# Layer 1's edge loop: the shrink of the running totals moved from VectorE to ScalarE, with reordered queues

## Chip, cores and metric

One core of a Trainium2 chip runs the whole kernel in one launch. The metric is the device time of one execution in microseconds (us); shorter is better. The kernel before takes 6182.91 us (median of 3 runs, 6182.76 to 6188.17).

## What is computed

The network has four layers, each a graph step and a feed-forward step, over 3125 nodes of width 256 and 50,000 edges sorted by destination. The change is in the edge part of layer 1's graph step, an attention over each node's incoming edges with 4 heads of 64 columns:

```python
e = x_l[src] + x_r[dst] + (ea @ W_e).reshape(-1, H, C)
e = jnp.where(e > 0, e, NEG_SLOPE * e)
logits = jnp.einsum('ehc,hc->eh', e, att)
m = jax.ops.segment_max(logits, dst, num_segments=N)
a = jnp.exp(logits - m[dst])
denom = jax.ops.segment_sum(a, dst, num_segments=N)
alpha = a / denom[dst]
out = jax.ops.segment_sum(x_l[src] * alpha[..., None], dst, num_segments=N)
```

The kernel does the maximum and the sums in one pass. It keeps a running maximum (a "top") and running totals per block of 128 destination nodes; when the top rises, the old total is multiplied by exp(old top - new top), its "shrink", before the new sum is added.

## The kernel before, in words

Edges come in 110 batches of 4 tiles of 128; a batch has two pairs of tiles, k = 0 and k = 1. `gat_edges` (L3294) writes one queue per engine with `skewed` (L1173): each engine goes through its list of steps once per iteration, and a step with lag n works on the batch of n iterations ago. An engine executes its list in the order in which it is written; semaphores tie the engines together. Layer 3 uses the same function with one head (`UNITS` is 1 there, 2 in layer 1).

The steps of one iteration before the change, by engine, with the batch that each works on where Q is the batch whose second top is raised:

- VectorE: `hot` (one-hot rows of two tiles, L1164, batch Q+3); tops of pair 0 (two reductions L3388, Q); `raise_first` (L3396, Q); join of pair 0 (L3637, Q+1); tops of pair 1 (L3388, Q); `raise_second` (L3403, L3405, L3408, Q), which writes the shrink exponents; join of pair 1 and both bends (L3637, L3642, Q+1); `add(0)` and `add(1)` (L3422, batch Q-1): four fused multiply-adds each, one per head, total[k] = total[1-k] * shrink + new sum; `late` (L3664, Q+1): the reductions that give the logits.
- TensorE: `turn_logits(1)` (L3464, L3467, Q), `add` (L3478, Q-1: the new sums), `spread` (L3484, L3486, Q: tops and logits spread over the edges), the edge products (L3627, L3628, Q+2), `turn_logits(0)` (Q+1), `turn` (L3449, Q+3).
- ScalarE: `shrinks` (L3513, Q), `weigh` (L3517, L3519, then sixteen multiplications L3528 with two copies L3531, Q), `turn` (L3508, L3509, Q+3), `flush` (L3544, L3545, Q-1).
- GpSimd: index cast and two one-hot tiles (L1154, L1156), four gathers (L1122), and the multiplication by `att` (L3659).

`spread` waits for `shrink_ready`, which `raise_second` raises; `weigh` waits for `spread_top`; `turn_logits(1)` waits for `topped`, since the tops of pair 0 must have read the two PSUM banks before they are filled again.

Of the kernel before, what the change touches and what calls it, by code (L numbers as in the profile page):

```python
# [12 lines left out]
ALU = mybir.AluOpType  # L13
ACT = mybir.ActivationFunctionType
AX = mybir.AxisListType

P = 128
# [11 lines left out]
BATCH = 4  # L29
# [157 lines left out]
def tiled(ap, width):  # L187
    return ap.rearrange("p (t d) -> p t d", d=width)
# [892 lines left out]
class Gather:  # L1081

    def __init__(self, s, net, placed, table, width, lo):
        self.net, self.placed, self.table, self.width, self.lo, self.n = net, placed, table, width, lo, placed.width - lo
# [61 lines left out]
    def hot_tiles(self, eng, q, i, b, tick):  # L1150
        eng.wait_ge(self.rec_loaded[b], i * 16 + 16)
        eng.wait_ge(self.hot_free, q + 1)
        eng.sem_inc(tick, 1)
        eng.tensor_copy(self.idx[b][:, :], self.column(b, self.placed.far)).then_inc(self.idx_ready, 1)  # L1154
        for k in range(BATCH // 2):
            ins = eng.tensor_scalar(at(self.onehot[b], k, P), self.net.columns[:, :], self.column(b, self.placed.near, k),  # L1156
                                    None, ALU.is_equal)
        ins.then_inc(self.hot_ready, 1)

    def hot_half(self, eng, q, i, b):  # L1160
        wide = [P, BATCH // 2, P]
        eng.wait_ge(self.rec_loaded[b], i * 16 + 16)
        eng.wait_ge(self.hot_free, q + 1)
        eng.tensor_tensor(tiled(self.onehot[b][:, :], P)[:, BATCH // 2:BATCH, :],  # L1164
                          self.net.columns[:, :].unsqueeze(1).to_broadcast(wide),
                          self.column(b, self.placed.near)[:, BATCH // 2:BATCH].unsqueeze(2).to_broadcast(wide), ALU.is_equal)\
            .then_inc(self.half_ready, 1)

    def wait_rows(self, eng, i, b):
# [2124 lines left out]
def gat_edges(net, name, heads, each, table, lo, logits_of, tops=None):  # L3294
# [11 lines left out]
    with ExitStack() as ctx:  # L3306
# [11 lines left out]
        power = [s.sb(f"power{b}", [P, KH]) for b in range(RING)]  # L3318
        weighted = s.sb("weighted", [P, BATCH * W])
        total = [s.sb(f"total{k}", [P, W]) for k in range(TWO)]  # L3320
        ps_hot = s.ps("ps_hot", [P, BATCH * P])
        ps_x = s.ps("ps_x", [P, TWO, 512])
        ps_row = s.ps("ps_row", [P, 2, 512])
# [11 lines left out]
        shrink_ready = s.sem("shrink_ready")  # L3335
        spread_top = s.sem("spread_top")
        eased = s.sem("eased")
        shrunk = s.sem("shrunk")
        powered = s.sem("powered")
        weighted_ready = s.sem("weighted_ready")  # L3340
# [21 lines left out]
        @block.vector  # L3362
        def _(dve):
            dve.memset(net.work[:, 0:NT * W], 0.0).then_inc(cleared, 1)
            dve.memset(top[:, :], -HUGE).then_inc(cleared, 1)
            dve.memset(total[TWO - 1][:, :], 0.0).then_inc(cleared, 1)
            if tops is not None:
                dve.memset(tops[:, :], -HUGE).then_inc(cleared, 1)
            dve.tensor_copy(ident[:, :], net.ident[:, :]).then_inc(ident_ready, 1)
            dve.tensor_scalar(minus[:, :], net.ident[:, :], -1.0, None, ALU.mult).then_inc(ident_ready, 1)  # L3370
            dve.tensor_scalar(fresh[:, :], placed.keep[:, :], -1.0, HUGE, ALU.add, ALU.mult).then_inc(fresh_step, 1)
            dve.sem_inc(topped, 2)
            dve.sem_inc(total_ready, TWO)
            dve.sem_inc(top_step, 1)
            logits.start_vector(dve)
            dve.wait_ge(cleared, 3 if tops is None else 4)
            dve.wait_ge(fresh_step, 1)

            def tops_of(k, h0):

                def step(q, i, b):
                    n = (q * TWO + k) * UNITS + h0 // 2
                    side = (k * UNITS + h0 // 2) % 2
                    dve.wait_ge(rows_turned, n + 1)
                    dve.wait_ge(topped, n + 1)
                    dve.sem_inc(dve_tick, 1)
                    w, c = min(2, heads - h0), k * heads + h0
                    dve.tensor_reduce(tile_top[:, c:c + w], tiled(ps_row[:, side, 0:w * PAIR], PAIR), AX.X, ALU.max)\  # L3388
                        .then_inc(topped, 1)
                return 4, step  # L3390

            def raise_first(q, i, b):
                n = q * TWO
                dve.wait_ge(topped, (n + 1) * UNITS + 2)
                dve.wait_ge(top_step, n + 1)
                dve.scalar_tensor_tensor(top_at(b, 0), top_at((b - 1) % RING, TWO - 1), fresh[:, bass.ds(n, 1)],  # L3396
                                         at(tile_top, 0, heads), ALU.add, ALU.max).then_inc(top_step, 1)

            def raise_second(q, i, b):
                n = q * TWO  # L3400
                dve.wait_ge(topped, (n + TWO) * UNITS + 2)
                dve.wait_ge(top_step, n + 2)
                dve.scalar_tensor_tensor(top_at(b, 1), top_at(b, 0), fresh[:, bass.ds(n + 1, 1)], at(tile_top, 1, heads),  # L3403
                                         ALU.add, ALU.max).then_inc(top_step, 1)
                dve.scalar_tensor_tensor(at(shrink[b], 0, heads), top_at((b - 1) % RING, TWO - 1), fresh[:, bass.ds(n, 1)],  # L3405
                                         top_at(b, 0), ALU.add, ALU.subtract).then_inc(shrink_ready, 1)
                dve.wait_ge(top_step, n + 3)
                dve.scalar_tensor_tensor(at(shrink[b], 1, heads), top_at(b, 0), fresh[:, bass.ds(n + 1, 1)], top_at(b, 1),  # L3408
                                         ALU.add, ALU.subtract).then_inc(shrink_ready, 1)

            def add(k):

                def step(q, i, b):
                    n = q * TWO + k
                    if k == 0:
                        dve.wait_ge(shrunk, q + 1)
                    dve.wait_ge(summed, n + TWO + 1)
                    dve.wait_ge(flushed, (n + 1) * FLUSH)
                    dve.wait_ge(total_ready, n + TWO)
                    for h in range(heads):  # L3420
                        own = slice(h * (each + 1), (h + 1) * (each + 1))
                        ins = dve.scalar_tensor_tensor(total[k][:, own], total[1 - k][:, own], shrink[b][:, k * heads + h:k * heads + h + 1],  # L3422
                                                       ps_s[:, k, own], ALU.mult, ALU.add)
                    ins.then_inc(total_ready, 1)
                return 5, step

            units = [tops_of(k, h0) for k in range(TWO) for h0 in range(0, heads, 2)]
            early, middle, late, find, hot = ((lag, lambda q, i, b, part=part: part(dve, q, i, b)) for lag, part in
                                              zip((3, 3, 3, 0, 1), logits.vector_steps()))
            ends = (add(0), add(1), late) if UNITS > 1 else (late, hot, add(0), add(1))  # L3430
            if UNITS > 1:
                skewed(dve, hot, *units[:UNITS], (4, raise_first), early, *units[UNITS:], (4, raise_second), middle, *ends)
            else:
                skewed(dve, find, *units, (4, raise_first), early, (4, raise_second), middle, *ends)

        @block.tensor
        def _(pe):
# [43 lines left out]
            def spread(q, i, b):  # L3481
# [3 lines left out]
                for m in range(BATCH):  # L3485
# [3 lines left out]
                ins.then_inc(spread_top, 1)  # L3489


            skewed(pe, *([(3, turn_logits(1))] if UNITS > 1 else []), (4, add), (1, lambda q, i, b: logits.blocks(pe, q)), (3, spread),
                   (1, lambda q, i, b: logits.tensor(pe, q, i, b)), (2, turn_logits(0)),
                   *([(2, turn_logits(1))] if UNITS == 1 else []), (0, turn))

        @block.scalar
        def _(act):
# [14 lines left out]
                act.wait_ge(shrink_ready, q * TWO + TWO)  # L3512
                act.activation(shrink[b][:, :], shrink[b][:, :], ACT.Exp).then_inc(shrunk, 1)  # L3513

            def weigh(q, i, b):
                act.wait_ge(spread_top, q + 1)
                act.activation(power[b][:, :], ps_fall[:, :], ACT.Relu).then_inc(eased, 1)  # L3517
                act.wait_ge(eased, q + 2)
                act.activation(power[b][:, :], power[b][:, :], ACT.Exp, scale=-1.0).then_inc(powered, 1)  # L3519
                g.wait_rows(act, i, b)  # L3520
                act.wait_ge(powered, q + 1)
                for k in range(TWO):
                    act.wait_ge(summed, q * TWO + k + 1)
                    for m in (2 * k, 2 * k + 1):
                        out = by_head(at(weighted, m, W), each + 1)
                        for h in range(heads):
                            lo = m * g.width + h * each
                            act.activation(out[:, h, 0:each], g.rows[b][:, lo:lo + each], ACT.Copy,  # L3528
                                           scale=power[b][:, m * heads + h:m * heads + h + 1])
                    ones = by_head(at(weighted, k, 2 * W), each + 1)[:, :, each]  # L3530
                    act.activation(ones, at(power[b], k, 2 * heads), ACT.Copy).then_inc(weighted_ready, 1)  # L3531
                act.wait_ge(weighted_ready, q * TWO + TWO)
                act.sem_inc(g.rows_free, 1)

# [9 lines left out]
                        act.activation(at(tops, blk, heads), top_at(b, k), ACT.Copy).then_inc(flushed, 1)  # L3544
                    act.activation(at(net.work, blk, W), total[k][:, :], ACT.Copy).then_inc(flushed, 1)  # L3545

            skewed(act, (3, shrinks), (3, weigh), (0, turn), (4, flush))


class L1Logits:  # L3550
# [943 lines left out]
```

## Time and profile before

| | us |
|---|---|
| median of 3 runs | 6182.91 |
| profiled execution | 6176.19 |
| its span, first to last instruction | 6174.6 |
| first to last shrink of layer 1 (109 steps) | 2226.7 to 3264.0 |

Busy share over the span: TensorE 81%, VectorE 66%, ScalarE 45%, GpSimd 50%. These are averages over stages with different limits; for this change only the stretch from 2227 to 3264 us counts. A timeline row gives the start, the time from the first to the end of the last of a run of equal instructions, the engine, the line, and in brackets how long the engine had been idle and what released it. Instructions of one engine overlap a little at their ends, so what one costs its engine is read from the distance between starts.

### The profile page before, as it was taken

The page shows a single profiled execution, that of the slowest core. Times are in us where ns is not written, and L with a number is a line of the kernel's source. Part 1 is how long each engine was busy: PE and PEld are TensorE (multiplying, and loading weights), DVE is VectorE, ACT ScalarE, POOL GpSimd, SP SyncE. Part 2 cuts the span into 40 slices and gives each one's busy share as a digit, 9 for nine tenths or more (in the row PEclk, how much of TensorE's full clock was granted, in tenths as well). Part 3 has the DMA queues.
Part 4 walks back from the last instruction along what each step waited for, and adds up shares of the span by engine and source line. Part 5 has one row for each costly group of instructions (what it writes and reads, how often), then busy time and mean ns, then how long its engine had stood idle before and what let it go on. Part 6 is the DMA issues. An engine that isn't in the chain of part 4 may idle for free. (4 is left out here: it accounts for less than half of the span.)

```text
span 6174.6 us, 119601 instructions
## 1 busy us (share of the span) xinstructions
PE 4978.6 (81%) x26396; PEld 3786.4 (61%) x26475; DVE 4081.7 (66%) x12578; ACT 2801.1 (45%) x8000; POOL 3087.3 (50%) x3487
## 2 busy tenths in 40 slices
PE   5720999998477779999993899969999997888695
PEld 4610677776354557777773677745657775777585
DVE  7771566665587779999996888754333336777612
ACT  0010777775115347777773111124533333787423
POOL 4787777775674068888880222213210002777221
PEclk9975999998696789999995999989989998999797
DMA  7521444445487222222231566544320002666453
GB/s 246 182 67 45 122 125 126 125 125 110 135 257 193 66 66 69 69 71 70 70 66 51 191 202 213 177 140 133 118 64 10 12 9 80 161 161 161 88 172 118
DMA packets 787155, 719.97 MB, mean 117 GB/s; under 512 B 349416, under 2 KB 693005, under 8 KB 786414
## 3 DMA queue, kind: packets, MB, share of 16 engines
q1 hardware_dynamic: 596376, 372.06, 21.2%
q0 software_dynamic: 120064, 280.26, 17.2%
q10 hardware_dynamic: 70486, 65.22, 3.0%
q8 instruction: 67, 1.10, 0.1%
q14 instruction: 162, 1.33, 0.1%
HBM read 520.74 MB, written 201.60 MB: 117 GB/s over the span
## 5 line engine op out<-in xcount | busy, mean ns | idle before, releaser
L1122 POOL DMA_INDIRECT l3e_rows<-table,l3e_idx x440 | 432.6, 983 | 733.8 <-DVE l3e_idx L1144 615.3
L1122 POOL DMA_INDIRECT l0e_rows<-table,l0e_idx x440 | 426.7, 970 | 154.3 <-issue 128.9
L1122 POOL DMA_INDIRECT l1e_rows<-table,l1e_idx x440 | 427.7, 972 | 121.4 <-issue 121.4
L890 POOL DMA_INDIRECT records_by_src<-l0n_rec_src,l0n_pos_at_src x390 | 398.0, 1020 | 115.4 <-issue 108.8
L3528 ACT ACTIVATE l1e_weighted<-l1e_rows,l1e_power 128x64 f32<-128x64 f32 x1760 | 442.6, 334 | 18.5 <-ACT l1e_power L3519 18.1
L1433 PE MATMUL l0e_ps_w<-l0e_wf,l0e_hidT 128*128 128x256 f32 x1760 | 435.3, 380 | 0.0
L3464 PE MATMUL l1e_ps_row<-net_ident,l1e_logit 128*128 128x128 f32 x1760 | 276.7, 280 | 82.4 <-DVE l1e_logit L3664 81.5
L1433 PEld LDWEIGHTS l0e_ps_w<-l0e_wf,l0e_hidT 128*128 128x128 f32 x1760 | 300.4, 191 | 63.0
L2168 ACT ACTIVATE l2fe_hT<-l2fe_ps_h,l2fe_own,l2fe_own 128x320 f32<-128x320 f32 x320 | 197.7, 618 | 310.7 <-PE l2fe_ps_h L2118 310.5
L3659 POOL TENSOR_TENSOR l1e_e<-l1e_e,l1x_att 128x512 f32<-128x512 f32 x220 | 313.8, 1446 | 29.2 <-DVE l1e_e L3642 21.5
L2827 ACT ACTIVATE l1fg_hT<-l1fg_ps_h,l1fg_b_cols 128x256 f32<-128x256 f32 x256 | 107.5, 471 | 458.0 <-PE l1fg_ps_h L2770 457.9
L1367 DVE SCALAR_TENSOR_TENSOR l0e_hidT<-l0e_ps_h,l0e_bf_low,l0e_raised 128x512 f32<-128x512 f32 x220 | 155.1, 746 | 227.6 <-ACT l0e_raised L1479 226.8
L2221 DVE SCALAR_TENSOR_TENSOR net_x<-l2fe_ps_y,l2fe_mix,net_x 128x256 f32 x200 | 96.7, 483 | 309.5 <-PE l2fe_ps_y L2130 309.5
L3388 DVE TENSOR_REDUCE l1e_tile_top<-l1e_ps_row 128x2 f32<-128x512 f32 x440 | 288.3, 685 | 16.1 <-PE l1e_ps_row L3467 3.5
L4057 PE MATMUL l2d_ps<-l2d_wide,net_work 128*128 128x512 f32 (+2 forms) x800 | 290.0, 518 | 8.6 <-DVE l2d_wide L4108 5.9
L3464 PEld LDWEIGHTS l1e_ps_row<-net_ident,l1e_logit 128*128 128x128 f32 x1760 | 191.6, 137 | 163.2 <-issue 110.7
L3478 PE MATMUL l3e_ps_s<-l3e_weighted,l3e_onehot 128*128 128x257 f32 x880 | 236.5, 414 | 53.1 <-ACT l3e_weighted L3531 52.6
L2951 POOL DMA_INDIRECT outputs<-l1fg_y,l1fg_target x64 | 66.3, 1035 | 404.0 <-DVE l1fg_y L2879 388.3
L3627 PE MATMUL l1e_ps_x<-l1x_xr,l1e_nodehot 128*128 x880 | 255.4, 392 | 2.8 <-ACT l1e_nodehot L3509 2.8
L2770 PE MATMUL l1fg_ps_h<-l1fg_xT,l1fg_w_in 128*128 128x256 f32 x1024 | 254.0, 381 | 0.8 <-issue 0.8
L3975 POOL DMA_DIRECT2D l2d_counts<-counts x192 | 107.1, 558 | 280.0 <-ACT l2d_wide L4167 139.9
L2784 PE MATMUL l1fg_ps_y<-l1fg_w_out,l1fg_hT 128*128 128x256 f32 x1024 | 241.5, 379 | 0.0
(857 smaller groups left out, 14927.0 us busy)
## 6 DMA issues: line engine op xcount, KB each, us to landing
counts<-l1f_total ACTq DMA_DIRECT2D x272, 128.0 KB, 4.4
l1fg_w_in<-in_L_ffn_W SPq DMA_DIRECT2D x32, 1024.0 KB
l1fg_w_out<-in_L_ffn_W SPq DMA_DIRECT2D x32, 1024.0 KB
records_by_dst<-l0n_blank_dst SPq DMA_DIRECT2D x5, 6512.0 KB
l3e_rec<-records_by_dst SPq DMA_DIRECT2D x110, 296.0 KB, 3.6
l2d_counts<-counts SPq DMA_DIRECT2D x208, 128.0 KB, 2.4
l2d_counts<-counts POOLq DMA_DIRECT2D x192, 128.0 KB
l3fg_w_in<-in_L_ffn_w SPq DMA_DIRECT2D x16, 1024.0 KB
```

Source lines behind the costliest of these rows:

```text
L890: pool.indirect_dma_start(self.to.records, bass.IndirectOffsetOnAxis(self.pos_at[b][:, j:j + 1], 0), at(self.rec[b], j, self.to.width), No ...
L1122: pool.indirect_dma_start(at(self.rows[b], k, self.width), None, self.table, bass.IndirectOffsetOnAxis(self.idx[b][:, k:k + 1], 0)).then_i ...
L1433: ins = pe.matmul(ps_w[:, k, m * D:(m + 1) * D], hidT[b][:, c * WIDE + (2 * k + m) * P:c * WIDE + (2 * k + m + 1) * P], at(wf2, c, D), sta ...
L2770: ins = pe.matmul(ps_h[:, n % HALVES, (m % 2) * SLICE:(m % 2 + 1) * SLICE], w_in[b][:, c * F + m * P:c * F + (m + 1) * P], at(xT[b], c, SL ...
L2784: ins = pe.matmul(ps_y[:, t, 0:D], hT[b][:, c * SLICE + t * P:c * SLICE + (t + 1) * P], at(w_out[b], c, D), start=c == 0, stop=c == FC - 1)
L3388: dve.tensor_reduce(tile_top[:, c:c + w], tiled(ps_row[:, side, 0:w * PAIR], PAIR), AX.X, ALU.max)\
L3464: pe.matmul(ps_row[:, side, lo:lo + P], logit[b][:, c:c + 1].to_broadcast([P, P]), net.ident[:, :], is_transpose=True, start=h == h0 and m ...
L3478: ins = pe.matmul(ps_s[:, k, 0:W], at(g.onehot[b], m, P), at(weighted, m, W), start=m == 2 * k, stop=m > 2 * k)
L3528: act.activation(out[:, h, 0:each], g.rows[b][:, lo:lo + each], ACT.Copy, scale=power[b][:, m * heads + h:m * heads + h + 1])
L3627: pe.matmul(out, at(self.nodehot[b], 2 * k + m, P), at(self.xr, self.block[k], D), start=True, stop=False)
L3659: pool.tensor_tensor(e, e, self.att[:, :].unsqueeze(1).to_broadcast([P, 2, D]), ALU.mult).then_inc(self.times_att, 1)
L4057: ins = pe.matmul(ps[0:k_in, n % 2, 0:width(g)], lhsT, wide[k % WIDE][:, 0:width(g)], start=t == 0, stop=False)
```

## The change

In layer 1 (`heads > 1`) the multiplication of a total by its shrink becomes a step of ScalarE, `fade(k)`: four activations, one per head, write total[1-k] * shrink into a new tile faded[k]. VectorE's `add(k)` is then one tensor_tensor over 260 columns, faded[k] + new sum. `fade(1)` stands at lag 4 between the two halves of the weighing of the next batch; `fade(0)` stands at lag 3 at the end of ScalarE's list. On VectorE the second join and both bends go directly behind the first join, ahead of the tops of pair 1; `add(0)`, `late`, `hot` and `add(1)` follow `raise_second` in this order. On TensorE the edge products go ahead of `spread`. GpSimd makes one one-hot tile instead of two and VectorE three instead of two. For one head (layer 3) the lists are the same as before.

```diff
-        for k in range(BATCH // 2):
+        for k in range(self.BY_POOL):            # BY_POOL = 1
...
-        eng.tensor_tensor(tiled(self.onehot[b][:, :], P)[:, BATCH // 2:BATCH, :],
+        eng.tensor_tensor(tiled(self.onehot[b][:, :], P)[:, self.BY_POOL:BATCH, :],
...
                 def step(q, i, b):
                     n = q * TWO + k
+                    if heads > 1:
+                        dve.wait_ge(faded_ready, n + 1)
+                        dve.wait_ge(summed, n + TWO + 1)
+                        dve.wait_ge(flushed, (n + 1) * FLUSH)
+                        dve.tensor_tensor(total[k][:, :], faded[k][:, :], ps_s[:, k, 0:W], ALU.add).then_inc(total_ready, 1)
+                        return
...
-            ends = (add(0), add(1), late) if UNITS > 1 else (late, hot, add(0), add(1))
             if UNITS > 1:
-                skewed(dve, hot, *units[:UNITS], (4, raise_first), early, *units[UNITS:], (4, raise_second), middle, *ends)
+                skewed(dve, *units[:UNITS], (4, raise_first), early, middle, *units[UNITS:], (4, raise_second), add(0), late, hot, add(1))
...
-            skewed(pe, *([(3, turn_logits(1))] if UNITS > 1 else []), (4, add), (1, lambda q, i, b: logits.blocks(pe, q)), (3, spread),
-                   (1, lambda q, i, b: logits.tensor(pe, q, i, b)), (2, turn_logits(0)),
-                   *([(2, turn_logits(1))] if UNITS == 1 else []), (0, turn))
+            blocks, products = (1, lambda q, i, b: logits.blocks(pe, q)), (1, lambda q, i, b: logits.tensor(pe, q, i, b))
+            if UNITS > 1:
+                skewed(pe, (3, turn_logits(1)), blocks, (4, add), products, (3, spread), (2, turn_logits(0)), (0, turn))
...
+            def fade(k):
+
+                def step(q, i, b):
+                    n = q * TWO + k
+                    if k == 0:
+                        act.wait_ge(shrunk, q + 1)
+                    act.wait_ge(total_ready, n + TWO)
+                    act.sem_inc(act_tick, 1)
+                    for h in range(heads):
+                        own = slice(h * (each + 1), (h + 1) * (each + 1))
+                        ins = act.activation(faded[k][:, own], total[1 - k][:, own], ACT.Copy,
+                                             scale=shrink[b][:, k * heads + h:k * heads + h + 1])
+                    ins.then_inc(faded_ready, 1)
+                return step
...
-            skewed(act, (3, shrinks), (3, weigh), (0, turn), (4, flush))
+            if heads > 1:
+                skewed(act, (3, shrinks), (3, weigh_first), (4, fade(1)), (3, weigh_second), (0, turn), (4, flush), (3, fade(0)))
```

`weigh_first` is the old `weigh` up to and with pair 0, `weigh_second` is pair 1 and the release of the gathered rows.

## Rows read from the trace of the kernel before

**Rows 1.** Instructions of one line: count, min/median/max ns, first and last start.
```profile
L3513 ACT ACTIVATE l1e_shrink<-l1e_shrink x110: 208/209/210, 2226.7 to 3264.0; 128x8 f32<-128x8 f32 x110
```
**Rows 2.** Busy time by stretch: PE, PEld, DVE, ACT, POOL, granted clock, DMA share, GB/s.
```profile
2600.00:2800.00 200.00, 181.30 (x1137) 141.61 (x1136) 187.52 (x485) 142.72 (x569) 173.51 (x190) 1.00 0.27 70
```
**Rows 3.** Timeline of VectorE in the middle of the loop.
```profile
2660.04 1.35 DVE L3388 TENSOR_REDUCE l1e_tile_top<-l1e_ps_row 128x2 f32<-128x512 f32 x2
2661.78 0.69 DVE L3637 TENSOR_TENSOR l1e_e<-l1e_ps_x,l1e_rows 128x512 f32<-128x512 f32 x1
2662.38 1.28 DVE L3388 TENSOR_REDUCE l1e_tile_top<-l1e_ps_row 128x2 f32<-128x512 f32 x2
2663.81 0.22 DVE L3403 SCALAR_TENSOR_TENSOR l1e_top<-l1e_top,l1e_fresh,l1e_tile_top 128x4 f32<-128x4 f32 x1
...
2664.08 0.22 DVE L3408 SCALAR_TENSOR_TENSOR l1e_shrink<-l1e_top,l1e_fresh 128x4 f32<-128x4 f32 x1
2664.22 0.68 DVE L3637 TENSOR_TENSOR l1e_e<-l1e_ps_x,l1e_rows 128x512 f32<-128x512 f32 x1
2664.82 1.28 DVE L3642 SCALAR_TENSOR_TENSOR l1e_e<-l1e_e 128x512 f32<-128x512 f32 x2
2666.02 1.82 DVE L3422 SCALAR_TENSOR_TENSOR l1e_total<-l1e_total,l1e_shrink,l1e_ps_s 128x65 f32<-128x65 f32 x8
2667.75 1.42 DVE L3664 TENSOR_REDUCE l1e_logit<-l1e_e 128x8 f32<-128x512 f32 x2
2669.09 0.42 DVE L1164 TENSOR_TENSOR l1e_onehot<-net_columns,l1e_rec 128x256 f32<-128x256 f32 x1
```
**Rows 4.** Timeline of ScalarE in the same stretch.
```profile
2664.33 0.21 ACT L3513 ACTIVATE l1e_shrink<-l1e_shrink 128x8 f32<-128x8 f32 x1 [0.80 <-DVE l1e_shrink L3408]
2665.67 0.18 ACT L3517 ACTIVATE l1e_power<-l1e_ps_fall 128x16 f32<-128x16 f32 x1 [1.13 <-PE l1e_ps_fall L3486]
2666.27 2.02 ACT L3528 ACTIVATE l1e_weighted<-l1e_rows,l1e_power 128x64 f32<-128x64 f32 x8 [0.17 <-ACT l1e_power L3519]
2668.20 0.20 ACT L3531 ACTIVATE l1e_weighted<-l1e_power 128x8 f32<-128x8 f32 x1
2668.30 2.00 ACT L3528 ACTIVATE l1e_weighted<-l1e_rows,l1e_power 128x64 f32<-128x64 f32 x8
2670.59 0.60 ACT L3508 ACTIVATE l1e_outside<-l1e_ps_hot 128x512 bf16<-128x512 f32 x1 [0.18 <-PE l1e_ps_hot L3449]
2672.71 0.41 ACT L3545 ACTIVATE net_work<-l1e_total 128x260 f32 x1
```
**Rows 5.** Timeline of TensorE in the same stretch.
```profile
2660.79 0.65 PE L3464 MATMUL l1e_ps_row<-net_ident,l1e_logit 128*128 128x128 f32 x4
2662.15 1.92 PE L3478 MATMUL l1e_ps_s<-l1e_weighted,l1e_onehot 128*128 128x260 f32 x8
2664.35 0.40 PE L3484 MATMUL l1e_ps_fall<-l1e_logit,l1e_minus 128*128 128x16 f32 x2 [0.29 <-DVE l1e_shrink L3408]
2665.49 0.68 PE L3627 MATMUL l1e_ps_x<-l1x_xr,l1e_nodehot 128*128 x2
2667.64 0.27 PE L3628 MATMUL l1e_ps_x<-l1e_we_parts,l1e_attrT 128*128 128x256 bf16 x1
2668.57 0.65 PE L3464 MATMUL l1e_ps_row<-net_ident,l1e_logit 128*128 128x128 f32 x4 [0.66 <-DVE l1e_logit L3664]
```
**Rows 6.** Timeline of GpSimd: the multiplication by the attention vector.
```profile
2665.59 2.87 POOL L3659 TENSOR_TENSOR l1e_e<-l1e_e,l1x_att 128x512 f32<-128x512 f32 x2 [0.25 <-DVE l1e_e L3642]
```
**Rows 7.** Timeline: TensorE's first instructions behind two idle gaps.
```profile
290.91 0.33 PE L818 MATMUL l0n_cell_ps<-l0n_cell_hot,l0n_cell_before 128*128 128x175 bf16 x1 [2.77 <-DVE l0n_cell_posf L726]
...
3257.93 1.11 PE L3464 MATMUL l1e_ps_row<-net_ident,l1e_logit 128*128 128x128 f32 x4 [2.88 <-DVE l1e_logit L3664]
```
**Rows 8.** Busy time by stretch, around and behind these gaps (columns as in Rows 2).
```profile
3258.00:3262.00 4.00, 3.88 (x18) 2.84 (x19) 2.31 (x5) 2.78 (x12) 0.00 (x0) 0.63 0.00 0
288.00:294.00 6.00, 3.23 (x23) 2.77 (x23) 4.64 (x29) 0.00 (x0) 4.62 (x8) 1.00 1.02 382
```

More of the change, by code:

```diff
@@ L1081 @@
 class Gather:
+    BY_POOL = 1
     def __init__(self, s, net, placed, table, width, lo):
@@ L1160, in hot_half @@
     def hot_half(self, eng, q, i, b):
[L1161 removed]
+        wide = [P, BATCH - self.BY_POOL, P]
         eng.wait_ge(self.rec_loaded[b], i * 16 + 16)
         eng.wait_ge(self.hot_free, q + 1)
[L1164 removed]
+        eng.tensor_tensor(tiled(self.onehot[b][:, :], P)[:, self.BY_POOL:BATCH, :],
                           self.net.columns[:, :].unsqueeze(1).to_broadcast(wide),
[L1166 removed]
+                          self.column(b, self.placed.near)[:, self.BY_POOL:BATCH].unsqueeze(2).to_broadcast(wide), ALU.is_equal)\
             .then_inc(self.half_ready, 1)
@@ L3320, in gat_edges @@
         total = [s.sb(f"total{k}", [P, W]) for k in range(TWO)]
+        faded = [s.sb(f"faded{k}", [P, W]) for k in range(TWO)]
         ps_hot = s.ps("ps_hot", [P, BATCH * P])
@@ L3337, in gat_edges @@
         eased = s.sem("eased")
+        faded_ready = s.sem("faded_ready")
         shrunk = s.sem("shrunk")
@@ L3429, in _ @@
                                               zip((3, 3, 3, 0, 1), logits.vector_steps()))
-            ends = (add(0), add(1), late) if UNITS > 1 else (late, hot, add(0), add(1))
             if UNITS > 1:
-                skewed(dve, hot, *units[:UNITS], (4, raise_first), early, *units[UNITS:], (4, raise_second), middle, *ends)
+                skewed(dve, *units[:UNITS], (4, raise_first), early, middle, *units[UNITS:], (4, raise_second), add(0), late, hot, add(1))
             else:
-                skewed(dve, find, *units, (4, raise_first), early, (4, raise_second), middle, *ends)
+                skewed(dve, find, *units, (4, raise_first), early, (4, raise_second), middle, late, hot, add(0), add(1))
         @block.tensor
@@ L3489, in spread @@
                 ins.then_inc(spread_top, 1)
-            skewed(pe, *([(3, turn_logits(1))] if UNITS > 1 else []), (4, add), (1, lambda q, i, b: logits.blocks(pe, q)), (3, spread),
-                   (1, lambda q, i, b: logits.tensor(pe, q, i, b)), (2, turn_logits(0)),
-                   *([(2, turn_logits(1))] if UNITS == 1 else []), (0, turn))
+            blocks, products = (1, lambda q, i, b: logits.blocks(pe, q)), (1, lambda q, i, b: logits.tensor(pe, q, i, b))
+            if UNITS > 1:
+                skewed(pe, (3, turn_logits(1)), blocks, (4, add), products, (3, spread), (2, turn_logits(0)), (0, turn))
+            else:
+                skewed(pe, (4, add), blocks, (3, spread), products, (2, turn_logits(0)), (2, turn_logits(1)), (0, turn))
         @block.scalar
@@ L3513, in shrinks, with weigh_first @@
                 act.activation(shrink[b][:, :], shrink[b][:, :], ACT.Exp).then_inc(shrunk, 1)
-            def weigh(q, i, b):
+            def fade(k):
[11 more added lines that the diff above has]
+                return step
+            def weigh_first(q, i, b):
                 act.wait_ge(spread_top, q + 1)
@@ L3521, in weigh, with weigh_pair @@
                 act.wait_ge(powered, q + 1)
-                for k in range(TWO):
+                weigh_pair(q, b, 0)
+            def weigh_pair(q, b, k):
                     act.wait_ge(summed, q * TWO + k + 1)
@@ L3531, in weigh, with weigh_second @@
                     act.activation(ones, at(power[b], k, 2 * heads), ACT.Copy).then_inc(weighted_ready, 1)
+            def weigh_second(q, i, b):
+                weigh_pair(q, b, 1)
                 act.wait_ge(weighted_ready, q * TWO + TWO)
@@ L3545, in flush @@
                     act.activation(at(net.work, blk, W), total[k][:, :], ACT.Copy).then_inc(flushed, 1)
-            skewed(act, (3, shrinks), (3, weigh), (0, turn), (4, flush))
+            if heads > 1:
+                skewed(act, (3, shrinks), (3, weigh_first), (4, fade(1)), (3, weigh_second), (0, turn), (4, flush), (3, fade(0)))
+            else:
+                skewed(act, (3, shrinks), (3, weigh_first), (3, weigh_second), (0, turn), (4, flush))
 class L1Logits:
```

## The prediction

> **What bounds the kernel now.** The page's chain of waits ends in the last microseconds of layer 3 and says nothing of this stage, so I went from the first and last instruction of a line, to the busy times by stretch, to the timelines of the single engines. One shrink runs per batch, the first at 2226.7 us and the last at 3264.0 [rows 1]: 1037.3 us for 109 steps, 9.52 us per batch. In that loop VectorE is busy 187.5 of 200 us, TensorE 181.3, GpSimd 173.5, ScalarE 142.7, and the granted clock is 1.00, that is 2.4 GHz [rows 2]. VectorE's timeline closes up without a gap that another engine ends [rows 3], so its instructions set the 9.52 us. ScalarE has gaps, the longest 1.13 us ahead of the first use of `spread`'s result [rows 4]. The reader should note the order in rows 4: shrink exponent, wait for TensorE, two small steps, eight weighings, eight weighings.
>
> **What VectorE saves.** The eight fused adds take it from 2666.02 to 2667.75, 1.73 us per batch [rows 3]. In their place stand two tensor_tensor over 260 columns. The trace has no such instruction; the one-hot over 256 columns takes 0.42 us, the join over 512 with a PSUM source 0.68, and their starts lie some 0.08 us closer than that (join to bend 0.60) [rows 3]. So one costs 0.34 to 0.60 us; I take 0.34, its neighbour by size. The wider one-hot (384 columns) lies between the same rows, 0.34 to 0.60; I take 0.47, 0.13 more than now. Together VectorE would need 1.73 - 0.68 - 0.13 = 0.92 us less, 8.60 us per batch, if it had nothing to wait for.
>
> **What the new waits do.** It has. Call Q the batch whose tops `raise_second` finishes in a VectorE iteration. `add(0)` and `add(1)` of that iteration belong to Q-1 (lag 5 against lag 4). `add(1)` waits for `fade(1)` of Q-1. On ScalarE this fade (lag 4) is written behind `shrinks` and `weigh_first` of Q (lag 3). `shrinks` of Q waits for `raise_second` of Q, and `weigh_first` waits for TensorE's `spread` of Q, which waits for the same. So within one iteration VectorE raises the top, then must wait until TensorE has spread it, ScalarE has weighed half a batch with it and faded the old total, and only then closes the iteration with `add(1)`. Queued behind `add(1)` is everything that leads to the next `raise_second`: tops, joins, bends. Before the change the add needed only the shrink exponent (ready 0.2 us after `raise_second`) and old sums. This is a closed loop through three engines, and its length is the new period if it exceeds 9.52 us.
>
> **Its length, from the start of `spread` (S = 0).**
> - To ScalarE's first use: 2664.35 [rows 5] to 2665.67 [rows 4], 1.32 us.
> - From there to the first weighing 0.60, and through eight weighings and the copy to the next group 2.03 [rows 4]: `fade(1)` starts at 3.95.
> - `fade(1)`: four activations of 65 columns. The row nearest is the weighing, 64 columns with the same kind of scale: eight start within 1.93 us (2666.27 to 2668.20), 0.24 each, and the run ends at 2.02, so the last lasts 0.33 [rows 4]. 3 x 0.24 + 0.33 = 1.06, bounded above by the 0.41 us flush of 260 columns taken four times, 1.64. Handing over costs about 0.05 (`raise_second` ends 2664.30, `spread` starts 2664.35) [rows 3, 5]. `add(1)` starts at 5.06, and the next tops at 5.40.
> - VectorE from the tops: tops of pair 0 and `raise_first` 1.74 (2660.04 to 2661.78), two joins 1.20, two bends 1.20 (2664.82 to 2666.02), tops of pair 1 1.43 (2662.38 to 2663.81), `raise_second` 0.49 [rows 3]: 6.06, and 0.05 to hand over. `spread` could start at 11.51.
> - TensorE from the tops: the second logits need the bank that the first top has read, 0.75 us after it starts (2660.04 [rows 3] to 2660.79 [rows 5]); the new sums start at +2.11 (2662.15). They are eight matmuls in 1.92; at a spacing of 0.22 the next matmul starts 1.76 after the first. The products, now ahead of `spread`, run from 2665.49 to 2667.64 and 0.11 to 0.27 more [rows 5]: 2.26 to 2.42. `spread` at +6.13, so at 11.53; with the upper ends 11.85. The moved products therefore just reach the path; left behind `spread` they would not be on it.
>
> So the period is 11.53 us at full clock, 2.01 more than now.
>
> **What is hidden.** `add(0)`, `late` and the wider one-hot follow `raise_second` and end about 2.2 us after it (0.34 + 1.34 + 0.47 [rows 3]), while `add(1)` waits to 5.06: some 2.9 us of cover. `late` needs GpSimd's products, two of 1.44 us [rows 6] from the first bend on; that bend now lies 3.2 us before `raise_second`, so they are done. GpSimd loses a one-hot tile and has ample time. ScalarE: `weigh_second` runs from about 4.9, then its old steps up to the last flush (2668.30 to 2673.12 [rows 4], 4.8 us with its waits), then `fade(0)`, 1.06: 10.8, ahead of the next `raise_second` at 11.4. This cover is 0.6 us; what ScalarE takes beyond it would lengthen the loop one for one.
>
> **The clock.** TensorE gets a gap. After `spread` (1.14) and the first logits (1.35) it transposes until about 3.1 and then waits for the bank at 5.40 + 0.75 = 6.15: 3.05 us idle per batch. Behind a gap of 2.88 us in this stage's own tail the first logits took 1.11 us instead of 0.65, and the next 4 us ran at a granted clock of 0.63, partly at 1.2 GHz [rows 7, 8]; behind one of 2.77 us in an earlier stage the clock stayed at 1.00 [rows 7, 8]. What falls away, (1 - 0.63) x 4 = 1.48 us, lies on TensorE's way to `spread`, which has 0.02 us to spare. I take two gaps of three as losing the clock: 0.99 us per batch, period 12.52 us. The bounds are none (11.53) and all (13.01).
> By the Trainium skill, page "TensorE: Matmul & The Clock Gate", section "HAM oscillation — how this bites in real kernels", an idle gap as short as this one would keep the clock; the sum would then be the one with none. The row at 3257.93 speaks against that rule.
>
> **The sum.** (12.52 - 9.52) x 110 = 330 us. The profiled execution took 6176 us (6174.6 span and some 1.6 around it), the median of the runs is 6183; on the median 6183 + 330 = 6513 us.
>
> **The rivals.**
> - *The clock holds.* The same loop without the loss: 11.53 to 11.85 us, 6183 + 221 to 256 = 6404 to 6439 us. For it: the gap at 290.91 us. Against it: the one at 3257.93, with this stage's own work.
> - *The clock falls at every gap*, or ScalarE runs beyond its 0.6 us: 13.0 us and a little more, 6567 to 6600 us.
> - *The other side: the fade is ready in time.* Were `add(1)` not held, VectorE would need 8.60 us, GpSimd at most its present 8.3 (173.5 / 200 x 9.52), ScalarE its present 6.8 and 8 x 0.24 = 1.9 more, 8.7 [rows 2, 4]. The period would be about 8.7 us: 6183 - 0.8 x 110, about 6095 us. It decides from the point at which the fade ends within 2.2 us of `raise_second`. The busy times of rows 2 allow it; the order of ScalarE's list does not, for spreading and half a weighing alone take 3.95.
> - *The loop is there but shorter*, because the parts overlap more than the starts show: 9.6 to 11.4 us, 6190 to 6390 us. Each step rests on a row in which the same two instructions follow each other, so I give it little.
>
> **Chances.** Some gaps lose the clock (6440 to 6567): 0.46; the clock holds: 0.25; every gap: 0.17; shorter loop: 0.06; faster: 0.05; within 0.2%, about 12 us and what a measurement can tell: 0.01. The range 6400 to 6590 takes in the first two and most of the third.
>
> **What would show it.** Right: 11.5 to 13 us between shrinks; VectorE idle nearly 3 us per batch, 300 us in all, ahead of the line of the adds, released by ScalarE's fade; eight more activations of 0.33 us per batch; TensorE idle about 3 us ahead of `turn_logits(1)`, released by the tops; a granted clock under 1.00 in the loop, or 1.00 for the first rival; layer 3's edges unchanged. Wrong: adds that start right behind the one-hot, or a spacing of shrinks under 9.5 us.

## The result and the profile after

The changed kernel takes 6625.93 us (median of 4 runs, 6624.03 to 6630.36), the kernel before, on the same chip, 6182.84 (4 runs). The ratio is 1.0719, with a 95% interval of 1.0704 to 1.0733: slower by 443 us. I had forecast slower by 330 us, 6400 to 6590 us. The direction and the loop came out, the size lies beyond the range.

The profiled execution took 6630.36 us, its span is 6628.5, 453.9 longer than before. The shrinks of the changed kernel (one line: count, min/median/max ns, first and last start):

```profile
L3521 ACT ACTIVATE l1e_shrink<-l1e_shrink x110: 208/209/210, 2231.9 to 3709.8; 128x8 f32<-128x8 f32 x110
```

Against [rows 1], 1477.9 us for 109 steps stand where 1037.3 stood: 13.56 us per batch instead of 9.52, and 440.6 of the 453.9 us. The rest is 5.2 us ahead of the loop and 8 behind it, which I did not trace. Busy time in the middle of the loop, columns as in [rows 2]:

```profile
2800.00:3000.00 200.00, 148.78 (x795) 116.67 (x793) 127.46 (x247) 127.87 (x517) 112.05 (x118) 0.85 0.19 49
```

No engine is busy for more than three quarters of it, and the granted clock is down from 1.00 to 0.85. A loop of waits is the bound. The waits from 2400 to 3400 us name its members (us in total, times, longest):

```profile
DVE l1e_total L3420 <- ACT l1e_faded L3533: 329.6, 73, 6.1
PE l1e_ps_row L3470 <- DVE l1e_tile_top L3389: 231.1, 73, 3.4
ACT l1e_power L3540 <- PE l1e_ps_fall L3492: 183.8, 73, 4.1
PE l1e_ps_s L3484 <- issue: 19.6, 44, 0.7
```

VectorE's adds wait for ScalarE's fade, ScalarE waits for `spread`, TensorE waits for the tops. One turn of the loop, first VectorE (start, us, engine, line; in brackets the idle time before and what ended it):

```profile
2814.08 0.55 DVE L1163 TENSOR_TENSOR l1e_onehot<-net_columns,l1e_rec 128x384 f32<-128x384 f32 x1
2818.94 0.42 DVE L3420 TENSOR_TENSOR l1e_total<-l1e_faded,l1e_ps_s 128x260 f32<-128x260 f32 x1 [4.30 <-ACT l1e_faded L3533]
2819.28 1.28 DVE L3389 TENSOR_REDUCE l1e_tile_top<-l1e_ps_row 128x2 f32<-128x512 f32 x2
2824.74 1.03 DVE L3404 SCALAR_TENSOR_TENSOR l1e_top<-l1e_top,l1e_fresh,l1e_tile_top 128x4 f32<-128x4 f32 x1
2825.95 0.41 DVE L3420 TENSOR_TENSOR l1e_total<-l1e_faded,l1e_ps_s 128x260 f32<-128x260 f32 x1
```

ScalarE in the same turn:

```profile
2815.23 0.18 ACT L3540 ACTIVATE l1e_power<-l1e_ps_fall 128x16 f32<-128x16 f32 x1 [2.35 <-PE l1e_ps_fall L3492]
2817.85 1.05 ACT L3533 ACTIVATE l1e_faded<-l1e_total,l1e_shrink 128x65 f32<-128x65 f32 x4
```

TensorE:

```profile
2814.01 0.29 PE L3490 MATMUL l1e_ps_fall<-l1e_logit,l1e_minus 128*128 128x16 f32 x2
2820.02 0.65 PE L3470 MATMUL l1e_ps_row<-net_ident,l1e_logit 128*128 128x128 f32 x4 [3.03 <-DVE l1e_tile_top L3389]
2822.29 3.81 PE L3484 MATMUL l1e_ps_s<-l1e_weighted,l1e_onehot 128*128 128x260 f32 x8 [0.71 <-issue]
2825.89 1.06 PE L3658 MATMUL l1e_ps_x<-l1x_xr,l1e_nodehot 128*128 x2
2828.65 0.60 PE L3658 MATMUL l1e_ps_x<-l1x_xr,l1e_nodehot 128*128 x2
2829.20 0.29 PE L3490 MATMUL l1e_ps_fall<-l1e_logit,l1e_minus 128*128 128x16 f32 x2
```

and GpSimd:

```profile
2822.88 2.86 POOL L3690 TENSOR_TENSOR l1e_e<-l1e_e,l1x_att 128x512 f32<-128x512 f32 x2 [2.38 <-DVE l1e_e L3673]
```

From the start of `spread` at 2814.01 the turn runs: ScalarE's first use at +1.22, `fade(1)` at +3.84, `add(1)` at +4.93, tops at +5.27. The forecast had 1.32, 3.95, 5.06 and 5.40. From the tops on it goes wrong: `spread` starts 9.92 us after them, not 6.1. The granted clock in that part (columns as in [rows 2]):

```profile
2817.00:2820.00 3.00, 0.00 (x0) 0.00 (x0) 1.06 (x3) 3.00 (x14) 2.34 (x3) 1.00 0.31 92
2820.00:2822.00 2.00, 1.56 (x10) 1.01 (x10) 1.87 (x4) 1.82 (x7) 0.50 (x1) 0.84 0.44 125
2822.00:2826.00 4.00, 3.71 (x9) 2.97 (x10) 3.86 (x9) 2.07 (x9) 2.86 (x2) 0.50 0.21 35
2826.00:2829.20 3.20, 3.20 (x14) 2.18 (x13) 2.02 (x5) 0.21 (x1) 0.00 (x0) 0.66 0.00 0
```

This turn, 15.19 us from `spread` to `spread`, is the longest of five that repeat in the trace; the others take 12.85 to 13.48. TensorE idles for 3.03 us and works on; then the granted clock falls to 0.50, 1.2 GHz, and the new sums take 3.81 us where they took 1.92 [rows 5].

### The profile page after: what moved, and what is told of

Read it like the earlier page. It is cut to its first block and busy times, and to the rows that moved or that the text cites. A ratio compares the mean times of both kernels' runs of the same rounds, so it can differ in the third digit from the quotient of the medians.

```text
span 6628.5 us, 119842 instructions
## 1 busy us (share of the span) xinstructions
PE 5159.2 (78%) x26396; PEld 3927.5 (59%) x26475; DVE 4074.3 (61%) x11918; ACT 3008.2 (45%) x8880; POOL 3020.5 (46%) x3377
## 5 line engine op out<-in xcount | busy, mean ns | idle before, releaser
L3470 PE MATMUL l1e_ps_row<-net_ident,l1e_logit 128*128 128x128 f32 x1760 | 321.8, 313 | 349.6 <-DVE l1e_tile_top L3389 342.3
L3470 PEld LDWEIGHTS l1e_ps_row<-net_ident,l1e_logit 128*128 128x128 f32 x1760 | 238.9, 160 | 405.3 <-DVE l1e_tile_top L3389 357.1
L3420 DVE TENSOR_TENSOR l1e_total<-l1e_faded,l1e_ps_s 128x260 f32<-128x260 f32 x220 | 92.5, 420 | 496.5 <-ACT l1e_faded L3533 495.2
L3484 PE MATMUL l1e_ps_s<-l1e_weighted,l1e_onehot 128*128 128x260 f32 x880 | 318.5, 523 | 31.5 <-issue 26.7
L3484 PEld LDWEIGHTS l1e_ps_s<-l1e_weighted,l1e_onehot 128*128 128x128 f32 x880 | 232.5, 276 | 126.0 <-issue 71.4
L3658 PE MATMUL l1e_ps_x<-l1x_xr,l1e_nodehot 128*128 x880 | 270.2, 409 | 2.7 <-ACT l1e_nodehot L3517 1.4
L1153 POOL CAST l1e_idx<-l1e_rec 128x4 int32<-128x4 f32 x110 | 34.3, 311 | 497.3 <-PE l1e_ps_fall L3492 261.5
```

The source lines that it names most:

```text
L3470: pe.matmul(ps_row[:, side, lo:lo + P], logit[b][:, c:c + 1].to_broadcast([P, P]), net.ident[:, :], is_transpose=True, start=h == h0 and m ...
L3484: ins = pe.matmul(ps_s[:, k, 0:W], at(g.onehot[b], m, P), at(weighted, m, W), start=m == 2 * k, stop=m > 2 * k)
L3658: pe.matmul(out, at(self.nodehot[b], 2 * k + m, P), at(self.xr, self.block[k], D), start=True, stop=False)
```

## The experiments

Eleven kernels ran. Medians stand against the kernel before on the same chip (6185.31, 6188.1 or 6184.83 us). Periods are the distance from the first to the last shrink over 109.

**Does the loop hold?** One step moved in ScalarE's list:

```diff
-skewed(act, (3, shrinks), (3, weigh_first), (4, fade(1)), (3, weigh_second), ...
+skewed(act, (4, fade(1)), (3, shrinks), (3, weigh_first), (3, weigh_second), ...
```

> The changed kernel with fade(1) first in ScalarE's list, ahead of shrinks and the first half of the weighing. Theory A (the loop raise_second, spread, half a weighing, fade(1), add(1) sets the period, 13.56 us now): the fade no longer stands behind spread, add(1) is ready 1.6 us after raise_second, and the period falls to what the engines need themselves, 9.3 us on VectorE (8.6 and 0.7 that raise_second waits while GpSimd multiplies), 9.5 to 10 on ScalarE: 6180 to 6240 us. Theory B (ScalarE's added work as such, eight more activations per batch, is what costs): the order does not matter, above 6500 us.

Measured: 6249.26 us, ratio 1.0107 (1.0090 to 1.0124), 10.07 us per batch, clock 1.00. The place of four activations in a list was worth 377 us: the loop is shown. But the time lies 9 us above the range put on record, the kernel is still 1% slower than before, and `raise_second`'s first instruction grew further. It ends with GpSimd's multiplication, 2810.03 against 2810.01 (timelines of VectorE and GpSimd in this run):

```profile
2808.00 2.03 DVE L3404 SCALAR_TENSOR_TENSOR l1e_top<-l1e_top,l1e_fresh,l1e_tile_top 128x4 f32<-128x4 f32 x1
2807.51 2.50 POOL L3690 TENSOR_TENSOR l1e_e<-l1e_e,l1x_att 128x512 f32<-128x512 f32 x2
```

**What does TensorE's list add?** In the changed kernel `blocks`, which loads registers for the products, stands between the second logits and the new sums; it was put behind the sums:

```diff
-skewed(pe, (3, turn_logits(1)), blocks, (4, add), products, (3, spread), ...
+skewed(pe, (3, turn_logits(1)), (4, add), blocks, products, (3, spread), ...
```

> The changed kernel with the register loads of TensorE (blocks) back behind the new sums. Theory A1 (in its trace TensorE stands 0.4 to 0.7 us between turn_logits(1) and the sums in most batches, because the loads now stand between them, and this lies on the way to spread): 0.4 to 0.7 us x 110 less, 6550 to 6585 us. Rival: the gap only takes up time that the sums would have spent at 1.2 GHz, or is a wait for the weighing: within 15 us of 6626.

Measured: 6551.72 us, ratio 1.0593 (1.0575 to 1.0611), 12.81 us per batch, clock 0.89 to 0.91. The time is as expected: 74 us for the place of a step that computes nothing. But the trace shows two things in it. Of the 77 turns between 2400 and 3400 us, 18 kept the full clock for 10 us and more behind a gap of TensorE as long as the others (3.03 to 3.37 us in both groups). One that kept it, with the granted clock behind it (columns as in [rows 2]), and the next, which did not:

```profile
2790.53 0.65 PE L3470 MATMUL l1e_ps_row<-net_ident,l1e_logit 128*128 128x128 f32 x4 [3.03 <-DVE l1e_tile_top L3389]
2790.53:2800.53 10.00, 8.51 (x54) 6.86 (x54) 7.73 (x15) 6.42 (x27) 6.08 (x7) 1.00 0.19 47
2802.78 1.11 PE L3470 MATMUL l1e_ps_row<-net_ident,l1e_logit 128*128 128x128 f32 x4 [3.04 <-DVE l1e_tile_top L3389]
```

The 18 turns take 12.26 us on average, the other 59 take 13.06. So of the 0.74 us per batch that this run gained, some 0.50 (13.56 - 13.06) went with the loads and the rest with the clock that was kept, an estimate from these means.

**Can the gap be avoided by order?** `spread` ahead of the products:

```diff
-skewed(pe, (3, turn_logits(1)), blocks, (4, add), products, (3, spread), ...
+skewed(pe, (3, turn_logits(1)), (4, add), blocks, (3, spread), products, ...
```

> The changed kernel with TensorE's list in the old order: sums, register loads, spread, edge products. Theory A (the products lie on the loop, 2.2 us at full clock and more at 1.2 GHz, and behind spread they fill the idle gap, so that the clock holds): the loop then closes over VectorE, 5.3 us from spread to the next tops and 6.7 from there to raise_second, period about 12.0 us, 6440 to 6480 us, granted clock near 1.00 in the loop. Rival (the products only moved into time in which TensorE waited anyway): within 30 us of 6626.

Measured: 6637.7 us, ratio 1.0737 (1.0719 to 1.0755), 13.61 us, clock 0.80 to 0.82. A miss for the theory; the rival's number holds (within 30 us of 6626). The gap only moved to a place ahead of `spread`, and there too the clock falls behind it (first two rows, TensorE; L3492 takes 1.03 us at full clock). And the products, now behind `spread`, hold up the logits of pair 0, for which the tops wait 0.77 us per batch (last row, VectorE):

```profile
2802.22 0.60 PE L3490 MATMUL l1e_ps_fall<-l1e_logit,l1e_minus 128*128 128x16 f32 x2 [2.84 <-DVE l1e_shrink L3409]
2802.66 1.85 PE L3492 MATMUL l1e_ps_fall<-l1e_top,l1e_nodehot 128*128 128x4 f32 x8
2809.73 1.36 DVE L3389 TENSOR_REDUCE l1e_tile_top<-l1e_ps_row 128x2 f32<-128x512 f32 x2 [0.89 <-PE l1e_ps_row L3473]
```

**What does the clock cost?** The gap was filled with matmuls that nobody reads, eleven and then six; in the third run the register loads also stood behind the sums:

```diff
+            def fill(q, i, b):
+                pe.wait_ge(eased, q + 2)
+                for _ in range(6):               # 11 in the first run
+                    pe.matmul(ps_fall[:, 256:512], net.ident[:, :], net.x[:, 0:256], start=True, stop=True)
...
-(2, turn_logits(0)), (0, turn))
+(2, turn_logits(0)), (0, turn), (3, fill))
```

> The changed kernel with eleven extra matmuls per batch (128x256 f32 into an unused part of the bank of ps_fall) in the 3 us in which TensorE waits for the first tops; nothing reads them. Theory A (about 2 us of the 13.56 are TensorE's clock at 1.2 GHz behind this gap): granted clock 0.97 to 1.00 in the loop and a period of 11.9 to 12.3 us, 6445 to 6490 us, although TensorE does 2.4 us more work per batch. Rival (the clock costs little, the excess is waits such as the register loads): no faster than 6600 us.

> As e4_gap_filled with six extra matmuls instead of eleven. Eleven ran as 22 passes of 0.22 us, 4.7 us, and pushed the logits 1.5 us past the tops; six take 2.6 and end before the tops are read. Theory A (the clock is worth about 2 us per batch): granted clock near 1.00 in the loop, period 11.9 to 12.1 us, 6440 to 6475 us. Rival (the clock is worth less, and e4 gained by hiding the register loads behind its own matmuls, as e2 did): 6540 to 6560 us.

> e5_gap_filled_6 with the register loads back behind the sums. Theory A1 (VectorE's part of the loop is now the longer one, 6.7 us from the tops to the end of raise_second, because raise_second waits some 0.8 us for GpSimd's multiplication to end): within 15 us of e5. Rival A2 (TensorE's part still closes the loop, and the loads add to it): 40 us or more below e5.

Measured: 6543.64 us (ratio 1.0580, 1.0562 to 1.0597) with eleven, 6500.94 (1.0510, 1.0492 to 1.0528) with six, 6488.08 (1.0490, 1.0473 to 1.0508) with six and the loads moved; 12.77, 12.37 and 12.27 us per batch, the clock 1.00 in all. With eleven, TensorE is busy for 200 of 200 us: the filling itself ran past the tops and held up the loop, and the time lies above the range put on record. With six:

```profile
2800.00:3000.00 200.00, 178.87 (x1066) 144.62 (x1065) 142.53 (x275) 138.96 (x562) 122.86 (x130) 1.00 0.21 53
```

More work on TensorE made the kernel 125 us faster. It still missed the 6440 to 6475 that a full clock was to give (and the rival's 6540 to 6560 too). With the clock up the loads were worth 13 us only, as was expected of the third run. With six, TensorE still stood 0.81 us between the second logits and the sums and reached `spread` 6.97 us after the tops (2802.31 against 2795.34); with the loads moved VectorE's branch took nearly as long. TensorE with six, then VectorE in the third run:

```profile
2810.83 1.99 PE L3484 MATMUL l1e_ps_s<-l1e_weighted,l1e_onehot 128*128 128x260 f32 x8 [0.81 <-issue]
```

```profile
2800.21 1.28 DVE L3389 TENSOR_REDUCE l1e_tile_top<-l1e_ps_row 128x2 f32<-128x512 f32 x2
2805.60 1.03 DVE L3404 SCALAR_TENSOR_TENSOR l1e_top<-l1e_top,l1e_fresh,l1e_tile_top 128x4 f32<-128x4 f32 x1
2812.20 0.42 DVE L3420 TENSOR_TENSOR l1e_total<-l1e_faded,l1e_ps_s 128x260 f32<-128x260 f32 x1 [3.31 <-ACT l1e_faded L3538]
2812.55 1.28 DVE L3389 TENSOR_REDUCE l1e_tile_top<-l1e_ps_row 128x2 f32<-128x512 f32 x2
```

and the row of TensorE that belongs to it:

```profile
2807.03 0.39 PE L3490 MATMUL l1e_ps_fall<-l1e_logit,l1e_minus 128*128 128x16 f32 x2 [0.60 <-DVE l1e_shrink L3409]
```

Tops at 2800.21, `spread` at 2807.03, tops at 2812.55: 6.82 + 5.52 = 12.34 us, where the forecast had 6.11 + 5.40. The 0.71 comes from `raise_second`, 1.03 us for an instruction of 0.22 [rows 3].

**What do the early bends cost by themselves?** The kernel before with this alone:

```diff
-skewed(dve, hot, *units[:UNITS], (4, raise_first), early, *units[UNITS:], (4, raise_second), middle, *ends)
+skewed(dve, hot, *units[:UNITS], (4, raise_first), early, middle, *units[UNITS:], (4, raise_second), *ends)
```

> The kernel before with one edit: the second join and the bends directly behind the first join, ahead of the tops of pair 1, as in the changed kernel; adds, fades and TensorE's list are as before. Theory C (an instruction of VectorE with two operands in SBUF waits until GpSimd's running tensor_tensor ends, and the new order puts raise_second into GpSimd's multiplication): raise_second's first instruction takes 1 to 2 us instead of 0.22, and since VectorE has no idle time here, 0.7 to 1.7 us x 110 more, 6260 to 6370 us. Rival (in the changed kernel that instruction only seemed long, by a wait on something else that is late there): 0.22 us, and within 20 us of 6183.

Measured: 6633.11 us, ratio 1.0725 (1.0707 to 1.0743), 13.58 us, clock 0.80 to 0.82. `raise_second` stood as expected (1.01 us), but the price was far above the 6260 to 6370 us put on record: a second loop, without any fade in it. Its waits from 2400 to 3200 us:

```profile
DVE l1e_tile_top L3388 <- PE l1e_ps_row L3467: 209.3, 59, 4.3
PE l1e_ps_fall L3484 <- DVE l1e_shrink L3408: 167.4, 59, 2.9
```

The tops wait for the logits of pair 0, these stand behind `spread` and the products in TensorE's list, and `spread` waits for `raise_second`, now late in VectorE's turn. TensorE idles 2.8 us ahead of `spread` and loses its clock too. If that reading holds, the products ahead of `spread` must open this loop:

```diff
-(4, add), blocks, (3, spread), products, (2, turn_logits(0)), ...
+(4, add), blocks, products, (3, spread), (2, turn_logits(0)), ...
```

> The kernel before with its second join and both bends directly behind the first join, and TensorE's edge products ahead of spread; fused adds and everything else as before. Theory D (with the bends early, the order spread, products, logits of pair 0 closes a loop raise_second to spread to products to logits to tops to raise_second, which cost the run with the bends early 4.1 us per batch): with the products ahead of spread they fall out of that loop, VectorE sets the period again with its 9.5 us and 0.8 us of raise_second behind GpSimd: 10.3 to 10.9 us, 6270 to 6340 us, raise_second still near 1.0 us, clock 0.95 or more. Rival (early bends cost as much by themselves, wherever the products stand): 13 us and more, 6560 to 6640 us.

Measured: 6302.82 us, ratio 1.0189 (1.0172 to 1.0206), 10.56 us, clock 0.96 to 0.97. As expected, a gain of 330 us. What is left over the 9.52 is chiefly `raise_second` on VectorE, now the bound (185 of 200 us busy); it ends at 2805.61, GpSimd's multiplication at 2805.60:

```profile
2804.58 1.03 DVE L3403 SCALAR_TENSOR_TENSOR l1e_top<-l1e_top,l1e_fresh,l1e_tile_top 128x4 f32<-128x4 f32 x1
2802.72 2.88 POOL L3660 TENSOR_TENSOR l1e_e<-l1e_e,l1x_att 128x512 f32<-128x512 f32 x2
```

**Is `raise_second` on the changed kernel's path?** The second join and the bends back behind it, nothing else:

```diff
-(4, raise_first), early, middle, *units[UNITS:], (4, raise_second), add(0), ...
+(4, raise_first), early, *units[UNITS:], (4, raise_second), middle, add(0), ...
```

> The change with one thing undone: the second join and both bends behind raise_second again. Theory B (in the change, TensorE's part from the tops to spread sets the loop, with the register loads and the low clock in it, and the wait of raise_second for GpSimd is hidden beside it): raise_second's first instruction is back near 0.22 us and nothing is gained, 13.1 to 13.7 us per batch, 6580 to 6640 us. Rival (the 0.8 us of raise_second lie on the loop): 12.5 to 12.9 us, 6510 to 6555 us.

Measured: 6625.68 us, ratio 1.0712 (1.0694 to 1.0730), 13.56 us: nothing gained, as expected, though the instruction is short again:

```profile
2820.68 0.22 DVE L3404 SCALAR_TENSOR_TENSOR l1e_top<-l1e_top,l1e_fresh,l1e_tile_top 128x4 f32<-128x4 f32 x1
```

With the low clock and the loads, TensorE's branch is the longer one and hides it. The same edit with the fade first:

> The change with both of its reorders of waits undone: fade(1) first in ScalarE's list (as in the run with the fade first) and, on VectorE, the second join and both bends behind raise_second again. Theory P (what kept the run with the fade first above the time before, 10.07 us per batch, is raise_second standing while GpSimd multiplies): raise_second's first instruction is back near 0.22 us, and the period falls below 9.52, to 9.0 to 9.5 us, since VectorE needs 8.6 and ScalarE 8.7 plus its hand-overs: 6125 to 6185 us. Rival (the excess was something else in the change: ScalarE's list now closes a loop of its own, or the tensor_tensor adds cost more than taken): 9.8 to 10.1 us, 6215 to 6250 us.

Measured: 6244.01 us, ratio 1.0092 (1.0075 to 1.0108), 10.05 us. `raise_second` is back at 0.22 us, VectorE busy for 159 of 200 us, and the period stays: my theory fell, the rival holds. ScalarE's own timeline gives the 10 us:

```profile
2802.47 1.05 ACT L3533 ACTIVATE l1e_faded<-l1e_total,l1e_shrink 128x65 f32<-128x65 f32 x4
2804.10 1.07 ACT L3533 ACTIVATE l1e_faded<-l1e_total,l1e_shrink 128x65 f32<-128x65 f32 x4 [0.58 <-DVE l1e_total L3420]
2805.76 2.02 ACT L3553 ACTIVATE l1e_weighted<-l1e_rows,l1e_power 128x64 f32<-128x64 f32 x8 [0.17 <-ACT l1e_power L3542]
2810.08 0.60 ACT L3516 ACTIVATE l1e_outside<-l1e_ps_hot 128x512 bf16<-128x512 f32 x1 [0.20 <-ACT l1e_weighted L3556]
2812.06 0.21 ACT L3572 ACTIVATE l_top<-l1e_top 128x4 f32 x1 [0.49 <-ACT net_work L3573]
2812.49 1.05 ACT L3533 ACTIVATE l1e_faded<-l1e_total,l1e_shrink 128x65 f32<-128x65 f32 x4
```

From `fade(0)` to `fade(0)` 10.02 us: some 8.6 of work and 1.44 of short waits (0.58 for `add(0)` between the two fades, 0.17, 0.20 and 0.49 for its own results). With two fades per batch in this order ScalarE is the bound. Without the 0.58 it would come to some 9.44 us, an estimate from these rows; no other order of two fades was run. A run made earlier, before this was known, had moved only one fade and kept TensorE's order of before (the lines are set against those of the kernel before):

```diff
-skewed(act, (3, shrinks), (3, weigh), (0, turn), (4, flush))
+skewed(act, (3, shrinks), (4, fade(0)), (3, weigh_first), (3, weigh_second), (0, turn), (4, flush))
...
-skewed(dve, hot, *units[:UNITS], (4, raise_first), early, *units[UNITS:], (4, raise_second), middle, *ends)
+skewed(dve, *units[:UNITS], (4, raise_first), *units[UNITS:], (4, raise_second), middle, add(0), add(1), first, (2, early[1]), second, hot)
```

`add(1)` is the fused one of before, `first` and `second` are the halves of `late`; the one-hot is split as in the change.

> A version without the loop and without that wait: the order of before on TensorE; only fade(0), directly behind shrinks where ScalarE waits for spread anyway; add(1) stays the fused form on VectorE; raise_second ahead of the bends as before; the reductions of late split, with the next batch's first join between them; one one-hot tile on GpSimd. By the theories VectorE needs 0.53 us less for the adds and 0.13 more for the one-hot per batch, GpSimd 0.7 less, ScalarE 0.97 more in a gap: period 9.1 to 9.2 us, 6135 to 6150 us. Rival (moving multiplications to ScalarE costs as such): not under 6180.

Measured: 6170.47 us (median of 10), ratio 0.9974 (0.9964 to 0.9983), 9.39 us per batch: faster than both kernels, by 0.26% over the one before. It is less than the 6135 to 6150 us expected: VectorE is still busy for 183 of 200 us, with new waits of 0.2 us. How much of the 0.13 us per batch comes from the fade and how much from the split `late` and the one-hot was not separated.

## Why the forecast was right, and where it failed

- **The loop**: right. `fade(1)` behind `weigh_first` closes it through three engines; moved ahead, it gives back 377 of 443 us.
- **From `spread` to the tops, 5.40**: right, 5.26 to 5.52. The prices taken from neighbours held: `fade` 1.06 against 1.05 to 1.07, the tensor_tensor 0.34 from start to start (2818.94 to 2819.28), and the wider one-hot 0.47 against 0.46.
- **From the tops to `spread`, 6.06 and 6.13**: the step that failed. Both branches were too short, and mending one alone would not have done: with the other still long the period hardly moves (13 us for the loads at full clock, nothing for `raise_second` at the low one). VectorE's priced `raise_second` by its row in an order in which GpSimd is not multiplying [rows 3, 6]; I moved the multiplication ahead of it and asked only whether `late` would find it done. The same rows showed the collision: the multiplication starts 0.77 us after the first bend and takes 2.87, so it ends at 3.64, while in the new order `raise_second` begins 1.20 + 1.43 = 2.63 us after that bend (3.2 stood in the forecast). TensorE's counted matmuls and left out the register loads, moved by the same line of the diff. At full clock the loop is 12.37 us (six matmuls in the gap), not 11.53: 0.84 of the 1.04 us by which the period was missed. The 18 turns that kept the clock by themselves, with the loads moved, agree: 12.26 us, against 12.27 with filling and loads moved.
- **The clock, two gaps of three, 0.99 us**: right in kind, low in size, in how many gaps lose the clock and in what one loses. All 15 gaps between 2600 and 2800 us, of 3.03 to 3.37 us, are followed by a stretch at 1.2 GHz (granted clock in windows of 2 us). The granted clock of 0.85 there is 30 us lost in 200, 2.0 per batch, twice the forecast. Of that, 1.19 us reach the period (13.56 - 12.37). This is the other 0.20. Some of the loss is covered: where the first logits already run slowly, the new sums start without the 0.71 us of idle time, as in the turn after the one above (TensorE):

```profile
2835.20 1.11 PE L3470 MATMUL l1e_ps_row<-net_ident,l1e_logit 128*128 128x128 f32 x4 [3.03 <-DVE l1e_tile_top L3389]
2837.81 2.23 PE L3484 MATMUL l1e_ps_s<-l1e_weighted,l1e_onehot 128*128 128x260 f32 x8
```

  The Trainium skill, page "TensorE: Matmul & The Clock Gate", section "HAM oscillation — how this bites in real kernels", warns only of idle gaps longer than these; by that rule such gaps would keep the clock. The trace contradicts it 15 times in those 200 us, and two of the experiments (`spread` ahead of the products, and the early bends alone) do so behind gaps of 2.75 to 2.92 us. Yet the run with the loads moved kept the clock behind 18 gaps of 3.03 to 3.37 us. So the length of a gap alone does not decide it, and neither the gap at 290.91, in another stage, nor the one at 3257.93 [rows 7] could tell how often this loop would lose the clock. What does decide it was not found.
- **The rivals**: the clock falling at every gap was the true one, but priced only up to 6600, with the same short branches. The other side, about 6095 us, was priced too low: with the fade in time the kernel takes 6244 to 6249, since ScalarE's 8.7 us of work were taken without the waits between its steps.
- **Hidden work**: right. `add(0)`, `late` and the one-hot end 2.0 us after `raise_second` (2814.63 against 2812.64), and `fade(0)` ends ahead of the next shrink. Layer 3 is unchanged: its shrinks spread over 571.0 us before and 571.4 after.
- **Not asked at all**: the second loop. With the bends early and the products behind `spread`, it costs 445 us by itself; the change's own move of the products opens it. I had called that move a cost of the path and had the products off it if left behind `spread`. The run with `spread` ahead of them shows that there they delay the tops, through the logits of pair 0, and the move is what keeps the early bends from being as dear as the fade.

How much of the 0.7 to 0.8 us at `issue` is the loads' own time and how much the sums' waits behind them was not separated.

## What to carry to other kernels

When a step moves to another engine, draw every closed loop through the lists, not only the one through the moved step, and price all its branches: the second longest sets the time as soon as the longest is mended. An instruction's duration holds for the neighbours on other engines that it had; where a move puts two engines on SBUF at once, ask for the price anew. An engine's share of busy time is no bound for its list: add the waits for its own results.

## What the runs showed of the hardware

- An instruction of VectorE with 128x4 operands took 0.22 us while GpSimd did not multiply and 1.01 to 2.03 in the turns shown when it ran into GpSimd's 128x512 multiplication, ending within 0.03 us of it in each pair read (in the changed kernel 2825.77 against 2825.74). The Trainium skill, page "SBUF — State Buffer", section "Who interferes with whom", states it: a VectorE instruction with two SBUF inputs contends with a GpSimd instruction that reads SBUF, and one of them blocks. The traces agree. The fused adds, with one of their two tensors in PSUM, kept their time: eight took 1.82 us beside the multiplication [rows 3, 6] and, in the run with early bends and products first, 1.85 just behind it:

```profile
2805.83 1.85 DVE L3422 SCALAR_TENSOR_TENSOR l1e_total<-l1e_total,l1e_shrink,l1e_ps_s 128x65 f32<-128x65 f32 x8
```

- TensorE's clock fell behind each of the 73 idle gaps of 3.03 to 3.37 us that the changed kernel has between 2400 and 3400 us, though the engine computed for some 10 us between two gaps. With one step of its list moved, it held behind 18 gaps of the same length and fell behind the rest. Within that run a turn that lost the clock took 0.80 us longer. Filling the gap with six useless matmuls brought it back to 1.00 and made the kernel 125 us faster.
- Register loads of a sequencer between two waits, which no row shows as busy, were worth 74 us in 110 batches by their place, part of it through the clock, and 13 us with the clock at 1.00.
